# Half-height score matmuls, keys projected one tile ahead, and the last step of an int8 rounding moved to GpSimd, in the two attention layers of a Trainium2 kernel

## The reference, cut to what matters

```
# layer 2: self attention, 16 heads of 16; one key and one value head shared, picked by a gate
gating = softmax(x @ W_gate.T); idx = argmax(gating)
q, k, v = split(x @ W_qkv.T)
k_shared = einsum('bth,bthd->btd', onehot(idx), k)
v_shared = einsum('bth,bthd->btd', onehot(idx) * max(gating), v)
att = softmax(where(causal, einsum('bhqd,bkd->bhqk', q, k_shared) / sqrt(hd), -inf))
y = einsum('bhqk,bkd->bhqd', att, v_shared)
# layer 3: cross attention with the context, int8 fake quantisation
q = qdq(x) @ qdq(wq).T + bq ;  k, v = split(cond @ wkv.T + bkv)
attn = softmax(einsum('bnhd,bmhd->bhnm', q, k) * scale)
o = einsum('bhnm,bmhd->bnhd', attn, v)
out = qdq(o) @ qdq(wp).T + bp        # qdq: s = max|x|/127 ; round(x/s) * s
```

## Time and profile before

| | |
|---|---|
| median of 3 runs | 787.84 us (785.68 to 791.85) |
| profiled execution, its own time | 787.84 us |
| its span, first to last instruction | 786.1 us |
| mean granted TensorE clock | 0.905 of full speed |
| self attention, first turn of x to the last tile's residual | about 74 to 166 us |
| cross attention, to the first residual tile of its output | about 157 to 229 us |

### The profile page before, as it was taken

One profiled execution on the slowest core, in us unless ns is written; L12 is line 12 of the kernel. 1 busy time (PEld: TensorE's weight loads), 2 busy tenths in 40 slices (PEclk: granted clock), 3 DMA queues, 4 the chain that ended last, 5 costly groups with the idle time before them and its releaser, 6 DMA issues.

```text
span 786.1 us, 11083 instructions
## 1 busy us (share of the span) xinstructions
PE 632.4 (80%) x3783; PEld 396.9 (50%) x3799; DVE 485.0 (62%) x1008; ACT 314.6 (40%) x534; POOL 241.4 (31%) x247
## 2 busy tenths in 40 slices
PE   1651879977971499999696998887999999999990
PEld 1341525544660135566444665554666666666660
DVE  6998688875979898887856877872122222212223
ACT  4910423415675058888644656402111111111110
POOL 3212065447911398730411312102211111111100
PEclk9675899998995569999997999979999999999996
DMA  8000402110006335641306005960000000000005
GB/s 268 0 0 17 158 0 69 31 38 1 1 1 130 92 78 145 183 118 58 108 1 281 1 1 226 389 281 28 28 27 28 27 27 24 23 26 27 20 15 167
DMA packets 32319, 61.72 MB, mean 79 GB/s; under 512 B 6233, under 2 KB 26713, under 8 KB 29945
## 3 DMA queue, kind: packets, MB, share of 16 engines
q1 hardware_dynamic: 24480, 48.93, 19.5%
q10 hardware_dynamic: 5632, 6.29, 2.2%
q0 software_dynamic: 2160, 5.90, 2.2%
HBM read 47.22 MB, written 13.50 MB: 77 GB/s over the span
## 4 chain that ended last, share of the span: by engine, by line
PE 54%; DVE 32%; issue 6%; POOL 3%; ACT 3%; DMA 2%; SPq 0%; DVEq 0%; POOLq 0%; ACTq 0%
PE bank L1907 18%; PE bank L1928 8%; PE bank L1485 4%; DVE region L1213 3%; PE bank L1126 2%; PE bank L1086 2%; PE bank L1918 2%; DVE XN L366 2%; PE bank L543 2%; PE bank L1110 2%; PE bank L571 2%; PE bank L1505 2%; DVE region L2217 2%; PE bank L507 2%; POOL rstd L380 1%
## 5 line engine op out<-in xcount | busy, mean ns | idle before, releaser
L1907 PE MATMUL bank<-region,wide 128*128 x368 | 142.3, 540 | 1.6 <-DVE etab L1766 1.6
L1786 DVE TENSOR_TENSOR wide<-wide,bank 128x448 f32<-128x448 f32 x46 | 28.5, 621 | 119.9 <-ACT wide L1834 119.9
L1907 PEld LDWEIGHTS bank<-region,wide 128*128 128x128 f32 x368 | 68.2, 190 | 61.6 <-issue 61.4
L1213 DVE TENSOR_REDUCE region<-bank 128x2 f32<-128x512 f32 x128 | 80.1, 680 | 6.9 <-PE bank L1086 6.3
L1684 POOL DMA_INDIRECT choice_results<-wide,to_row x23 | 22.7, 986 | 182.9 <-DVE wide L1799 182.9
L1928 PE MATMUL bank<-region,XN 128*128 x322 | 73.4, 380 | 1.2 <-DVE wide L1799 1.2
L1149 ACT ACTIVATE region<-bank 128x1024 f32<-128x1024 f32 x64 | 62.9, 1024 | 15.8 <-PE bank L1110 15.6
L1834 ACT ACTIVATE wide<-bank 128x448 f32<-128x448 f32 x46 | 24.9, 543 | 106.2 <-PE bank L1907 106.2
L1928 PEld LDWEIGHTS bank<-region,XN 128*128 128x128 f32 x322 | 59.6, 190 | 9.2 <-issue 2.1
L1086 PE MATMUL bank<-region 128*128 128x256 bf16 x256 | 51.9, 304 | 9.0 <-DVE region L1213 6.1
L380 POOL TENSOR_TENSOR rstd<-vareps,half_neg 128x4 f32<-128x4 f32 x16 | 18.3, 1146 | 119.0 <-DVE vareps L376 119.0
(11 more groups left out here) (306 smaller groups left out, 1230.9 us busy)
## 6 DMA issues: line engine op xcount, KB each, us to landing
region<-in_L_ffn_experts_dram SPq DMA_DIRECT2D x8, 2688.0 KB, 15.7
region<-ctx_parts SPq DMA_DIRECT2D x24, 192.0 KB
region<-norm_parts SPq DMA_DIRECT2D x24, 192.0 KB
channel_values<-wide ACTq DMA_DIRECT2D x8, 512.0 KB, 3.8
ctx_parts<-region SPq DMA_DIRECT2D x40, 64.0 KB, 2.0
region<-in_L_ffn_w_gate_up_dram SPq DMA_DIRECT2D x4, 512.0 KB, 6.2
wide<-channel_values SPq DMA_DIRECT2D x16, 128.0 KB, 2.5
norm_parts<-region SPq DMA_DIRECT2D x24, 64.0 KB, 3.3
```

Of the source, the lines that this page charges most:

```text
L1213: e.tensor_reduce(nmax[i % 2][:, at_:at_ + KC], score_bank("scores", n).rearrange("p (c n) -> p c n", c=KC), AX.X, ALU.max, negate=True).t ...
L1786: e.tensor_tensor(HB8[par][:, cols], silu8[:, cols], bank[hf][:, 512:512 + I8 // 2], ALU.mult)\
L1907: last = e.matmul(bank[hf][:, 512 * gu:512 * gu + hw], xbT[par][:, P * c:P * c + P], region[:, bass.ds(off + (2 * gu + c) * I8 + hw * hf, ...
```

## The change: what it does

- **Scores.** The key blocks hold 4 heads instead of 8, with a mask that serves both halves of the partitions: heads of the upper 64 channels and of the lower 64 share the columns. A score matmul now takes 64 partitions (one half, r) and 64 weight columns (one sequence, b), and 256 columns. There are 8 of them a tile instead of 4. The two partition halves write to different banks. In self attention both causal matmuls come first.
- **Key blocks.** `kbd` multiplies 512 elements a partition instead of 1024, once a tile in self attention and twice in cross attention.
- **Order in self attention.** `key_value` runs one tile ahead: tiles 0 and 1 ahead of the loop, and step t ends with tile t+1. Each half's gate logits follow that half's turn; the second half of the queries is projected in step 1.
- **Gate.** The reciprocal sum is folded into a second one-hot plane, so the scaling of the value half (L761) is gone from each tile; one multiplication is added once.
- **Turned probabilities.** ACT empties the whole double bank in self attention; DVE's copy (L781, seven tiles) is gone.
- **Ternary weights.** ACT casts two pieces ahead of the loop and one in each of steps 2 to 5. DVE sums two pieces in step 1, two at the end of self attention, two in step 2 of cross attention.
- **Cross attention's output.** DVE writes the rounded value with the constant still in it into XN (from PSUM, `out_rounded`). For tiles 0 to 6 POOL subtracts the constant and multiplies by the scale, in place; for tile 7 DVE does. `values` waits for `out_rounded`. The transposes of the output still wait for the scaled tiles.

```
+        HL = HC // 2
+        PAIR_AT = (0, 1, 4, 5, 2, 3, 6, 7)
+        KBD = [[carve(HL, P) for _ in range(KC)] for _ in range(2)]
...
# pool_attention, s == 1
                for i in range(NT):
                    if i >= 2:
                        kbd(i)
                    e.tensor_tensor(V[:, i, :], V[:, i, :], bvrow, ALU.add).then_inc(s_att["v_ready"], 1)
                    e.wait_ge(s_att["v_ready"], i + 1)
+                    if i >= 3:
+                        scaled_out(i - 3)
                    if i >= 2:
                        pool_blank_keys(e, ch, i - 2)
                for i in range(NT):
+                    if i % 2 == 1 and i // 2 + NT - 3 < NT - 1:
+                        scaled_out(i // 2 + NT - 3)
...
+        def scale_out(e, i, done="out_quantised"):
+            xi = XN[:, D * i:D * i + D]
+            e.tensor_scalar(xi, xi, MAGIC, out_scale(i)[:, 1:2], ALU.subtract, ALU.mult).then_inc(s_att[done], 1)
+            def scaled_out(i):
+                e.wait_ge(s_att["out_rounded"], i + 1)
+                scale_out(e, i)
+                e.wait_ge(s_att["out_quantised"], i + 1)
...
# pe_attention, scores(i)
+                if s == 0:
+                    for r in range(2):
+                        e.matmul(sbank(i)[:, 512 * r:512 * r + 512], identb[:, :], causal..., start=True, stop=False)
                for c in range(KC):
+                    for r in range(2):
+                        lane = slice(P // 2 * r, P // 2 * r + P // 2)
+                        at_ = 512 * r + HL * T * c
+                        for b in range(2):
+                            last = e.matmul(sbank(i)[T * b:T * b + T, at_:at_ + HL * T],
+                                            QT[lane, c, P * i + T * b:P * i + T * b + T],
+                                            KBD[i % 2][0 if s == 0 else c][lane, :, T * b:T * b + T], ...)
...
# pe_attention, ahead of and in the loop, s == 0
+                turn_half(XN, 0, 0); gate_logits(0); key_value(0)
+                turn_half(XN, 1, KC); gate_logits(1); key_value(1)
+                project_half(wqkvT, 0, XT, 0, 0, s_att["q_in_psum"])
...
-                if s == 0 and 1 <= t < NT:
-                    key_value(t)
+                if s == 0 and t == 1:
+                    project_half(wqkvT, 0, XT, 1, KC, s_att["q_in_psum"])
+                if s == 0 and 2 <= t < NT - 1:
+                    if t == 2:
+                        key_value(t)
+                    key_value(t + 1)
...
# vec_attention
-            ch.link(e.tensor_scalar(src, src, sc[:, 2:3], MAGIC, ALU.mult, ALU.add))
-            return e.tensor_scalar(dst..., src, MAGIC, sc[:, 1:2], ALU.subtract, ALU.mult)
+            return e.tensor_scalar(dst..., src, sc[:, 2:3], MAGIC, ALU.mult, ALU.add)
...
-                e.tensor_scalar(SEL[:, i, HD:2 * HD], SEL[:, i, HD:2 * HD], gate_rec[:, i:i + 1], None, ALU.mult)
...
-                e.tensor_copy(PT[:, 512:1024], bank[1][:, 512:1024]).then_inc(s_att["probs_T_vector"], 1)
...
+                    for c in range(2):            # step 1, self attention
                         vec_ternary_sums(e, ch, c)
+                    for c in range(2, 4):         # step NT + 3, self attention
+                        vec_ternary_sums(e, ch, c)
+                    for c in range(4, TW // TCH): # step 2, cross attention
+                        vec_ternary_sums(e, ch, c)
```

More of the change, by code:

```diff
@@ L179, in program @@
         gate_exp = carve(NT, H)
-        gate_hot = carve(NT, H)
+        gate_hot = carve(NT, 2, H)
         gate_max, gate_pick, gate_sum, gate_rec = (carve(NT) for _ in range(4))
-        KBD = [[carve(HC, P) for _ in range(KC)] for _ in range(2)]
+        HL = HC // 2
+        PAIR_AT = (0, 1, 4, 5, 2, 3, 6, 7)
+        KBD = [[carve(HL, P) for _ in range(KC)] for _ in range(2)]
         wide = sb("wide", [P, 22 * D])
@@ L397, in quantise_in_psum @@
             ch.link(e.reciprocal(sc[:, 2:3], sc[:, 1:2]))
[L398 to L399 removed]
+            return e.tensor_scalar(dst.rearrange("p (h d) -> p h d", d=HD), src, sc[:, 2:3], MAGIC, ALU.mult, ALU.add)
         def round_f8(e, ch, v, m, out_):
@@ L536, in scores @@
                         e.wait_ge(s_att["scores_shifted"], NT * s + i - 1)
+                if s == 0:
+                    for r in range(2):
+                        e.matmul(sbank(i)[:, 512 * r:512 * r + 512], identb[:, :], causal.rearrange("p a b -> p (a b)"),
+                                 start=True, stop=False, skip_group_check=True)
                 for c in range(KC):
[L538 to L546, removed]
+                    for r in range(2):
[4 more added lines that the diff above has]
+                                            QT[lane, c, P * i + T * b:P * i + T * b + T],
+                                            KBD[i % 2][0 if s == 0 else c][lane, :, T * b:T * b + T],
+                                            start=(s == 1), stop=True, skip_group_check=(s == 0))
                 last.then_inc(s_att["scores_made"], 1)
@@ L570, in values @@
                     for j in range(8):
-                        last = e.matmul(ps(4 + i % 2, w * j, w * j + w)[T * b:T * b + T, :],
-                                        PT[:, P * j + T * b:P * j + T * b + T], VBD[i % 2][:, b, 0 if s == 0 else j, :],
+                        k = PAIR_AT[j]
+                        last = e.matmul(ps(4 + i % 2, w * k, w * k + w)[T * b:T * b + T, :],
+                                        PT[:, P * j + T * b:P * j + T * b + T], VBD[i % 2][:, b, 0 if s == 0 else k, :],
                                         start=True, stop=True)
@@ L576, in pe_attention @@
             if s == 0:
+                e.wait_ge(s_xn, NT + 4)
+                turn_half(XN, 0, 0)
+                gate_logits(0)
                 key_value(0)
-                gate_logits(0)
-                for hf in range(2):
-                    e.wait_ge(s_turned, TURN["att0"] + KC * (hf + 1))
-                    if hf == 1:
-                        gate_logits(1)
-                    project_half(wqkvT, 0, XT, hf, KC * hf, s_att["q_in_psum"])
+                e.wait_ge(s_xn, 2 * NT)
+                turn_half(XN, 1, KC)
+                gate_logits(1)
+                key_value(1)
+                project_half(wqkvT, 0, XT, 0, 0, s_att["q_in_psum"])
             def warm(n):
@@ L697, in act_attention @@
                         f(t - lag)
+                if s == 0 and t == 1:
+                    leave_half(QT, 1, KC, s_att["q_in_psum"], s_att["q_ready"])
+                if s == 0 and 2 <= t < TW // TCH:
+                    act_ternary_cast(e, t)
                 if s == 0 and t == NT + 2:
@@ L809, in vec_attention @@
                     select(t)
-                if s == 0 and t == 0:
-                    for c in range(TW // TCH):
+                if s == 0 and t == 1:
+                    for c in range(2):
                         vec_ternary_sums(e, ch, c)
```

70 lines of the change are left out of this document (33 added, 37 removed).

## The result

The changed kernel takes 781.17 us (median of 4 runs, 773.01 to 781.42) beside 786.76 us for the kernel before; the ratio on record is 0.9877, 95% interval 0.9844 to 0.9911 (the two medians alone would give 0.993, since the changed kernel's times stand in two groups). The forecast was 767, range 761 to 775. The four times are not spread evenly: 781.17, 781.42, 781.18 and 773.01. So five of ten runs stand near 781 and five near 773. That gap of 8 us turns out to be the larger part of what was mispredicted.

What follows compares the result with a forecast made beforehand. TensorE was taken to bound self attention, with VectorE close behind, and VectorE to carry cross attention's chain. Gains 10.7 + 6.5 + 1.1 + 2.6 = 20.9 us, from 787.8 to 766.9; range 761 to 775.

Steps and rivals of the forecast that it cites:

- Score matmuls, 1.0 us: Each tile's eight half-height score matmuls take 1.0 us as a group; with both mask matmuls 1.54 instead of 2.65.
- Rivals 1 and 2: Score matmuls overlap only as column pairs, not row halves (775, chance 0.08); all eight run one after another (796, chance 0.04).
- The 0.3 us more a tile: Score matmuls: estimated cost if the second channel half's weight loads were exposed, 2 to 3 us in all.
- Steady self attention, 6.25 us a tile: TensorE's self-attention tile falls from 7.36 to 6.25 us and TensorE still bounds, by only 0.1.
- Gain 6.5 us: Self attention, third tile's scores to eighth maximum: 31.3 us instead of 37.8.
- Gain 10.7: In front of the steady self-attention tiles: third scores start at 104.0 instead of 114.67; 1.9 less if the clock rises late.
- End of self attention, 1.1: Gain of 1.1 us there: 0.6 from the dropped copy, 0.5 from normalisation at 170.5 instead of 171.02.
- Gain 2.6: Cross attention: gains of 1.1, 0.8 and 2.1 us, less 1.4 lost at the memset before the eighth scores.
- I take 0.6: Cross attention: GpSimd's scaling of a tile takes 0.6 us, between 0.40 for one input and 0.74 for two.
- The high end of my chain, 4.7: Cross attention: VectorE's rounding through GpSimd to scores takes 4.7 us instead of 3.9, with blocks of 1.32 and scaling 0.74.
- Rival 3: TensorE, less busy, loses its clock in cross attention: six tiles of 7.4 us instead of 4.4, total 785, chance 0.03.
- Behind it all is released by what comes before: After cross attention: experts' loads are in time, and only the last results' long DMA wait is in the chain.

Runs made afterwards that it cites:

- e1: The changed kernel again, no edit, for a second trace and its spread: 773.78 us median, 772.35 to 781.09, ratio 0.9843.
- e9: e6 with 46 unused matmuls while TensorE waits for the last turn of the first layer's result: 767.42 us, ratio 0.9740.
- e2: The changed kernel with both GpSimd memsets moved ahead of the loop of cross attention: 771.91 us, ratio 0.9802.
- e4: The changed kernel with memsets ahead of the cross-attention loop and the eighth selection ahead of the fourth tile's normalisation: 769.93 us, ratio 0.9774.
- e6: As e4, but both memsets at the end of GpSimd's part of self attention: 768.27 us, ratio 0.9751.
- e7: The changed kernel, but VectorE scales all eight cross-attention tiles itself, GpSimd none: 775.18 us, ratio 0.9832.
- e10: e6 with GpSimd's scaling undone, so VectorE scales all tiles: 770.82 us, ratio 0.9792.
- e8: The kernel before with only the half-height scores and key blocks of the change: 787.76 us, ratio 0.9977.
- e5: The changed kernel with unused matmuls filling TensorE's waits: 6 before the eighth key's turn, 11 before the eighth cross scores; 774.51 us, ratio 0.9813.

## Why the prediction was wrong, step by step

- **Score matmuls, 1.0 us: right**, 1.09 as a group and 1.02 to the next issue. The row of four column groups was a good stand-in for two row and two column halves. Rivals 1 and 2 fall. The 0.3 us more a tile, an estimate by the Trainium skill's page "TensorE: Matmul & The Clock Gate", Part 3, is not what the trace shows.
- **Steady self attention, 6.25 us a tile: right** (6.24 in the changed kernel). **"Gain 6.5 us" was mis-sized**: 29.7 forecast, 30.0 in e1 but 33.1 in the profiled run. The wait for the eighth key's turn was in the forecast; that the clock may fall behind it was put at nothing. This is 3.4 us in the profiled run, 0.3 in e1.
- **In front, "Gain 10.7": mis-sized.** 105.7 forecast for the third maximum, 109.2 found. I let the clock rise at 79.8; it rose at 84.1 and was low again from 87.5 to 90.9. I had priced a late rise at 1.9 us; the stage came out 3.5 us long. e9, with the clock up in front, puts the gates where the forecast had them and takes 2.5 us off the third maximum, so about that much is the clock; the other 1.0 stays open, with half clock twice in that stage of e9 too.
- **End of self attention, 1.1: right**, 1.5 measured.
- **Cross attention, "Gain 2.6": wrong sign in the profiled run** (22.5 + 21.0 + 15.9 = 59.4 against 57.9, a loss of 1.5; 55.7, a gain of 2.2, in e1). Two terms failed: the scaling's length, and the clock behind the wait at the memset, put at nothing. "I take 0.6" for the scaling: 1.15, outside my bounds of 0.40 and 0.74, because the rows that set them hold no tensor_scalar with a constant and a column of scales. So tiles took 4.70 and 4.43 us by turns instead of 4.38: in those of 4.70 VectorE waited 0.22 us for scores that had waited for GpSimd's block. The wait at the memset was 2.4 us for TensorE, and the eighth maximum came 1.9 us late in e1 (6.3 us behind the seventh), not 1.4. The high end of my chain, 4.7, was the better number, but by luck: it came from longer blocks, and they took the 1.0 that I had forecast. The Trainium skill's page "GPSIMD Engine Reference", section "Elementwise — side-by-side cycle accounting", by which the forecast had an estimated 0.2 us plus dispatch, doesn't agree with the 1.15 us of this trace.
- **Rival 3, "TensorE, less busy, loses its clock in cross attention", was given 0.03** on the argument that 72% busy at full clock is on record. A mean over 16.7 us doesn't show the waits inside it. In the changed kernel the clock fell not in the steady tiles (e2, e4, e6 and e9 run theirs at full clock) but behind the wait in front of the last one, and it costs 3.4 us, not 18. The rival as written isn't refuted either: with 4.9 us tiles the clock did fall at their end in e7 and e10, for 3.4 us (in e8, with the same tiles, it stayed up). Between the two traces of one kernel the stretches behind the two waits are 6.5 us. The other runs have no trace, so that each run near 781 has both stretches is inferred from e2 to e5.
- **"Behind it all is released by what comes before": right as to waits, but not as to time.** From the first residual to the end it is 557.2 us before, 560.5 after, 561.6 in e1, 555.7 in e4, with nothing edited there. TensorE's half-clock stretches in it differ from trace to trace (after the change 227.5 to 254.8 and 258.2 to 278.7, and three between 493.7 and 538.1; before 236.8 to 288.0 and 516.7 to 527.0). The same instructions in both traces show where the 3.3 us arise. The normalisation that starts at 500.66 before and at 488.42 after is 271.8 us behind the first residual before and 269.7 after, so up to there the changed kernel is 2.1 us faster; the next one, at 510.82 and 500.07, has lost 1.5 of that (281.9 and 281.4), and the other 3.8 us come later. So the loss lies where the changed kernel has its three late stretches. No run moved these stretches alone, so that they are the cause is read from place and clock, not tested; why they differ between traces stays open.

The sum, against the profiled run: 3.5 in front, 3.4 at the eighth key, 4.1 in cross attention (22.8 + 19.0 + 13.5 = 55.3 against 59.4), 3.3 behind, less 0.4 at the end of self attention: 14 us, from 20.9 to the 6.9 us that the span lost. The step that failed is the same in most of them: the forecast let TensorE run at full clock in front (but for 1.9 us), behind the two waits and in the later layers, and gave a loss of the clock 0.03. The traces show half-clock stretches in each of these places, and those behind the two waits are 6.5 of the 14 us. With the two waits out of the way, e6 is at 768.27 us, inside the range, and beats both kernels.

## What to carry to other kernels

When a change makes TensorE's work shorter, look for the one step of the loop in which it will now wait, not at its mean busy share: a wait of 1.6 us cost 3.1 us more in matmuls at half clock behind it here, in some runs and not in others. Before giving GpSimd a step that a faster engine's next input is queued behind, write down everything that its queue holds between the two, memsets too, and move what has no reader yet into a hole of that queue. A shorter matmul is worth nothing in a tile where the next one waits for a chain that started in the same step (e8). And one trace of a kernel whose times stand in two groups tells only about one of them: take a second before you explain a stage.

## What the runs showed of the hardware

- Eight f32 matmuls of 64 rows, 64 weight columns and 256 columns, over both row halves and both column halves, 16 records: 1.09 us, the same as two of 128 rows, 64 weight columns and 512 columns.
- GpSimd's tensor_scalar on 128x256 f32, with a constant and a per-partition scale, in place: 1.15 us (mean of seven); the same instruction on VectorE 0.42 (mean of eight, e7). A two-input addition of that size is 0.73 on GpSimd. Of 1024 and 512 elements, the key block is 1.90 and 1.04 us.
- VectorE's tensor_scalar from SBUF into SBUF was held until a GpSimd memset had ended: one of 128x256 f32 took 1.97 us instead of 0.41 beside a memset of 1.83 (e2), one of 128x4 took 1.81 instead of 0.17 beside one of 1.80 (e6). One that read PSUM was not held: 0.48 us beside a memset. Two ternary sums took 2.34 us with a memset beside them (e2) and without (e6).
- After TensorE had waited 1.55 us, the granted clock fell to half for 6.8 us in one trace and not in another of the same kernel; after 2.40 us, for 10.3 us and not at all. After 0.94 us it fell for 3.4 us in one trace (e9) of five.
